# New orders of work for the filling, the steady rounds and the emptying of a three-stage, four-lane decoder kernel

## The chip, the cores and the metric

The kernel runs on one core of one Trainium2 chip. The metric is the device time of the launch in microseconds (us); the kernel before has a median of 3741.29 us over 3 runs (3738.55 to 3749.99). The core has a tensor engine (PE; PEld is its weight load), a vector engine (DVE), a scalar engine (ACT), a GpSimd engine (POOL) and a sync engine (SP) that here only waits, clears semaphores and issues DMAs. Each engine runs its own instructions strictly in order; an instruction that waits on a semaphore holds back all behind it on that engine.

## The reference

32 sequences of 112 tokens with 256 features pass through two pre-norm decoder layers, in fp32. Cut to what matters:

```python
x = x + attn0(layernorm(x))          # 16 heads of 16, 4 key heads, rope, rms norm, tanh-capped causal softmax
x = x + xattn0(layernorm(x), ctx)    # 16 heads of 64 over ctx, causal mask: only ctx rows 0..111 count
x = x + ffn0(layernorm(x))           # 256 -> 1024 gelu -> 256, plus a low-rank term from tokens 1..16
x = x + attn1(layernorm(x))          # 8 heads of 128, latent keys and values of 32
x = x + xattn1(layernorm(x), ctx)    # 16 heads of 16 over 375 ctx rows, with a mask
x = x + moe(layernorm(x))            # 4 experts, top 2 of a gate on the mean over tokens; each expert is a
                                     # whole encoder layer (attention, layernorm, 256->1024->256, layernorm)
```

## The kernel before, in words

**Three stages.** Stage 1 does attn0 and xattn0, stage 2 does ffn0, attn1, xattn1 and the gate, stage 3 first routes (which expert takes which sequence) and then does the 64 expert items. Between stages all engines meet: stage 2 cannot start before the last sequence of stage 1 is done, since weights and buffers are laid over each other.

**Four lanes.** In each stage four lanes work at the same time, called A, B, C and D here (`s` = 0, 1, 2, 3), each with its own buffers, its own two PSUM banks and its own semaphores. A lane does one sequence (a batch) after the other: 8 each in stages 1 and 2, 16 items each in stage 3. Inside a batch nearly every step depends on the one before, and the steps go from engine to engine (a product on PE, a copy or exp on ACT, a mask or a norm on DVE, an inverse root on POOL, and so on). One lane alone therefore leaves each engine idle most of the time; four lanes fill one another's gaps.

**Pieces.** For every engine and stage there is a generator `batch(s, at)`, and each `yield` in it ends a piece: stage 1 has 25 pieces on PE, 19 on ACT, 19 on DVE, 3 on POOL and 4 on SP; stage 2 has 41, 27, 23, 5 and 5; stage 3 has 14, 11, 10, 3 and 4. "A16" on PE is piece 16 of lane A there. Of the pieces that the prediction names: in stage 2 PE 8 and 9 are key products (L892), PE 10 a value product (L827, 8 records), PE 16 the output product of attn1, PE 17 the transposes (L814) that wait for DVE 10 (layernorm's normalise, L1156), PE 19 to 26 the eight pairs of score products of xattn1 (L952), each followed by a masked maximum on DVE (L1232), PE 28 to 35 the second scores (L968, L971), exp on ACT (L1085) and the product with the values, PE 40 the gate. DVE 9 is the residual and layernorm after attn1 and DVE 0 starts the next batch: it waits for `go`, which SP gives after the batch's last DMA has landed. In stage 3 PE 1 is the qkv product (L1465), which waits for the expert's weights (`c_in`); PE 10 and 11 are the first layer of the expert's hidden part, PE 12 and 13 the second (L1536); DVE 0 needs PE 1 and SP's `go_last`, DVE 8 is the layernorm after PE 13, DVE 9 the item's output. SP 2 clears the lane's semaphores after DVE 8, gives `go` and, where the next item has another expert, loads its weights; if not, it only raises `c_in`. SP 3 does the same for `go_last` and the row parameters after POOL 2, the output DMA.

**The order.** `run_slots` (L133) interleaves the pieces of the lanes for one engine. A round has 1000 turns. `TURNS` (L59) gives each piece a turn within its batch, and `lead` says how far ahead each lane is: in stage 1 (0, 250, 500, 750), in stage 2 (0, 341, 505, 677), in stage 3 (0, 262, 500, 762). Turns are only an order: no time is waited for. A hardware loop (`Fori`, count - 1 times: 7, 7 and 15) holds one round of four lanes, starting at the turn 0 of lane A. Before it stands the filling: the same table from turn -750 (stage 1) to 0, so lane D begins alone, C joins at -500, B at -250. Behind it stands the emptying: the same table once more with nothing new begun for the leading lanes, so D ends at turn 250, C at 500, B at 750, and A runs on alone to 1000. Filling and emptying are straight code. Together a stage is filling (1.5 batches of work in stage 1), rounds of 4 batches, and emptying (2.5 batches).

Of the kernel before, what the change touches and what calls it, by code (L numbers as in the profile page):

```python
# [40 lines left out]
def offsets(parts):  # L41
    at, out = 0, {}
    for name, w in parts:
# [17 lines left out]
    "sp1": ((51, 993, 998, 999,),) * 4,  # L61
    "pe1": ((3, 47, 53, 128, 128, 183, 212, 230, 307, 329, 393, 393, 432, 451, 463, 526, 549, 576, 591, 697, 725, 756, 847, 891, 915,),) * 4,
    "act1": ((68, 121, 170, 231, 289, 320, 401, 410, 410, 410, 437, 483, 574, 687, 751, 770, 840, 915, 915,),) * 4,
    "dve1": ((39, 96, 96, 212, 212, 264, 361, 405, 429, 495, 541, 550, 630, 631, 699, 725, 817, 875, 964,),) * 4,
    "pool1": ((79, 276, 739,),) * 4,
# [42 lines left out]
}  # L108


class Tally:


# [12 lines left out]
class Place:  # L126


    def __init__(self, n, last=False):
        self.n, self.last = n, last  # L130


def run_slots(eng, lanes, count, batch, turns, lead):  # L133

# [1699 lines left out]
```

## Time and profile before

| | us |
|---|---|
| median of 3 runs | 3741.29 (3738.55 to 3749.99) |
| the profiled execution | 3746.19 |
| its span, first to last instruction | 3744.5 |
| around the span | 1.7 |
| mean granted TensorE clock | 0.953 of full |
| PE busy | 3393.0 (91%) |
| DVE, ACT, POOL busy | 2125.9 (57%), 1948.2 (52%), 377.1 (10%) |

The profile is one execution. Busy time of PE counts a matmul at the half clock twice as long as at the full one, so it is no measure of work done. Stage 1 lies at 27 to 967 us of the span, stage 2 at 1004 to 2531, the routing at 2531 to 2578, stage 3 at 2578 to the end.

### The profile page before, as it was taken

How to read it: one execution, taken by the hardware profiler on the slowest of the kernel's cores; microseconds unless marked ns; L12 is line 12 of the kernel's file. 1: busy time of each engine (PE TensorE's matmuls, PEld its weight loads, DVE VectorE, ACT ScalarE, POOL GpSimd, SP SyncE). 2: the span in 40 equal slices, each digit the busy share in tenths (PEclk: the TensorE clock that was granted, in tenths of full speed). 3: DMA queues.
4: the chain of work that ended last, by engine and by line, in shares of the span. 5: the costliest groups of instructions: out<-in, count | busy, mean ns of one | idle time of the engine just before them, and what ended most of it. 6: DMA issues, size and time to landing. Idle time of an engine off the chain costs nothing. (4 is left out here: it accounts for less than half of the span.)

```text
span 3744.5 us, 81272 instructions
## 1 busy us (share of the span) xinstructions
PE 3393.0 (91%) x30471; PEld 2533.5 (68%) x30471; DVE 2125.9 (57%) x6898; ACT 1948.2 (52%) x6531; POOL 377.1 (10%) x455
## 2 busy tenths in 40 slices
PE   6999999998699899999999999973999989999997
PEld 4777777776466565656565656633887877877886
DVE  3666666666255454545455554522666666766765
ACT  2555555555144444444444444422666666666664
POOL 1111111111000000000000000000111111111111
PEclk8999999999699999999999999965999999999998
DMA  2000000000200000000000000004000011010000
GB/s 78 13 12 16 12 12 16 12 16 6 90 17 17 21 17 21 17 21 17 23 14 23 14 24 14 7 6 174 15 11 12 16 52 53 16 52 12 16 11 10
DMA packets 63549, 94.38 MB, mean 25 GB/s; under 512 B 7762, under 2 KB 59602, under 8 KB 62146
## 3 DMA queue, kind: packets, MB, share of 16 engines
q1 hardware_dynamic: 55074, 83.41, 7.0%
q0 software_dynamic: 8224, 7.36, 1.7%
q8 instruction: 190, 3.11, 0.3%
q14 instruction: 61, 0.50, 0.0%
HBM read 72.07 MB, written 18.37 MB: 24 GB/s over the span
## 5 line engine op out<-in xcount | busy, mean ns | idle before, releaser
L1232 DVE CUSTOM_DVE_ANT_0 PON<-pps,PMR 112x375 f32<-112x375 f32 x512 | 259.9, 545 | 305.8 <-PE pps L952 304.9
L1465 PE MATMUL bps<-BXT,Bwexp 128*128 128x112 f32 x3072 | 382.2, 283 | 26.7 <-SPq L1386 12.7
L1465 PEld LDWEIGHTS bps<-BXT,Bwexp 128*128 128x128 f32 x3072 | 369.2, 198 | 46.1 <-ACT BXT L1554 16.8
L1571 ACT ACTIVATE BPT<-bps,Blow 112x112 f32<-112x112 f32 x1024 | 346.8, 381 | 38.4 <-DVE Blow L1686 38.4
L1085 ACT ACTIVATE PPT<-pps,mcol 125x896 f32<-125x896 f32 x192 | 193.0, 1005 | 198.9 <-PE pps L971 198.6
L1571 ACT ACTIVATION_READ_ACCUMULATOR BPT<-bps,Blow 112x1 f32 x1024 | 241.1, 235 | 0.0
L952 PE MATMUL pps<-PKT,PQM 64*112 64x375 f32 x1024 | 227.1, 521 | 10.0 <-DVE Pmx L1232 7.9
L1536 PE MATMUL bps<-Bwexp,BPT 128*112 128x256 f32 x1024 | 235.2, 381 | 0.1
L655 POOL TENSOR_TENSOR rstd<-var,nhalf 112x1 f32<-112x1 f32 (+1 forms) x96 | 148.3, 1545 | 771.3 <-DVE var L573 535.2
L1265 POOL TENSOR_TENSOR Prstd<-Pvar,nhalf 112x1 f32<-112x1 f32 x128 | 71.6, 560 | 1450.8 <-DVE Pvar L1152 1450.8
L498 ACT ACTIVATE PT<-PT,low 112x112 f32<-112x112 f32 x512 | 191.2, 387 | 43.5 <-DVE low L630 43.3
L1536 PEld LDWEIGHTS bps<-Bwexp,BPT 128*112 128x112 f32 x1024 | 176.3, 176 | 43.1 <-ACT BPT L1594 3.4
L971 PE MATMUL pps<-PQM,PKT 64*125 64x448 f32 x768 | 195.0, 587 | 0.0
L1160 DVE TENSOR_TENSOR PX<-PX,pps 112x256 f32<-112x256 f32 x96 | 40.3, 420 | 269.4 <-PE pps L827 124.9
L1594 ACT ACTIVATE BPT<-bps,Bwexp 128x112 f32<-128x112 f32 x512 | 140.1, 390 | 70.5 <-PE bps L1465 70.5
L1727 POOL TENSOR_TENSOR Brstd<-Bvar,nhalf 112x1 f32<-112x1 f32 x128 | 78.5, 613 | 895.9 <-DVE Bvar L1658 895.9
L1493 PE MATMUL bps<-BKT,BQM 64*112 64x112 f32 x2048 | 137.7, 275 | 20.9 <-ACT BPT L1571 20.1
L1685 DVE TENSOR_REDUCE Bmx<-bps 112x8 f32<-112x896 f32 x128 | 138.9, 1086 | 13.5 <-PE bps L1493 13.3
L1493 PEld LDWEIGHTS bps<-BKT,BQM 64*112 64x112 f32 x2048 | 114.5, 179 | 47.0 <-ACT BPT L1571 23.3
L1690 DVE TENSOR_TENSOR BPT<-BPT,Brec 112x896 f32<-112x896 f32 x128 | 139.8, 1092 | 4.4
L329 PEld LDWEIGHTS ps<-CT,wa_sb 128*128 128x128 f32 x1024 | 132.3, 206 | 11.1 <-ACT CT L455 1.4
L952 PEld LDWEIGHTS pps<-PKT,PQM 64*112 64x112 f32 x1024 | 76.6, 175 | 91.6 <-issue 64.1
(287 smaller groups left out, 7442.3 us busy)
## 6 DMA issues: line engine op xcount, KB each, us to landing
Bwexp<-in_we SPq DMA_DIRECT2D x7, 2304.0 KB, 13.8
PCX<-in_ctx SPq DMA_DIRECT2D x32, 375.0 KB
BXIN<-xmid SPq DMA_DIRECT2D x64, 112.0 KB
out<-BY POOLq DMA_DIRECT2D x64, 112.0 KB, 2.9
Bwexp<-in_we SPq DMA_DIRECT2D x7, 777.0 KB, 4.5
wa_sb<-in_wa SPq DMA_DIRECT2D x1, 4736.0 KB, 14.4
Brexp<-in_re SPq DMA_DIRECT2D x7, 672.0 KB
XIN<-in_x SPq DMA_DIRECT2D x32, 112.0 KB
```

The lines of the kernel that those rows point to most:

```text
L498: m = A(PT[s][:, h, :], PT[s][:, h, :], ACT.Exp, bias=low[s][:, h:h + 1], accum_out=sums[s][:, h:h + 1])
L655: g.tensor_tensor(rstd[s][:, 0:n], var[s][:, 0:n], nhalf[0:T, 0:n], ALU.pow).then_inc(rstd_ready[s], 1)
L952: m = mm(bank[s][i][0:T, 0:LC], QM[s][side[i], r // 4, r % 4, :], KT[s][side[i], r // 4, :], start=True, stop=True)
L971: m = mm(bank[s][i][0:KP, 0:QW], KT[s][side[i], c, k * KP:(k + 1) * KP], QM[s][side[i], c, :, :], start=False, stop=True, skip_group_check ...
L1085: A(PT[s][0:KP, k, :, :].rearrange("p (i v) q -> p i (v q)", i=2), PS[s][0:KP, :, 0:QW], ACT.Exp, bias=mcol[:, k, bass.ds(at.n[s] + s * qu ...
L1232: m = v.tensor_tensor_reduce(out=ON[s][0:T, i * LC:(i + 1) * LC], in0=bank[s][i][0:T, 0:LC], in1=MR[s][:, :], scale=1.0, scalar=-3.0e38, o ...
L1465: m = mm(o[:, j * T:(j + 1) * T], wt[:, c, n0 + j * 128:n0 + (j + 1) * 128], rhs[:, c, :], start=(c == 0), stop=(c == 1))
L1493: m = mm(bank[s][i][0:T, v * T:(v + 1) * T], QM[s][side[i], c, v, :], KT[s][side[i], c, :], start=True, stop=True)
L1536: m = mm(b0[0:T, 0:D], HT[s][:, mt, :], W(s, "l2", FT)[:, mt, :], start=(mt == 0), stop=(mt == FT - 1))
L1571: m = A(PT[s][0:T, h, :], bank[s][i][0:T, v * T:(v + 1) * T], ACT.Exp, scale=0.25, bias=low[s][:, h:h + 1], accum_out=sums[s][:, h:h + 1])
L1594: m = A(HT[s][:, mt, :], bank[s][g][:, j * T:(j + 1) * T], ACT.Relu, bias=wc(s, "b1")[:, mt:mt + 1])
L1690: v.tensor_tensor(PT[s][0:T, eight, :], PT[s][0:T, eight, :], rec[s][:, eight].unsqueeze(2).to_broadcast((T, 8, T)), ALU.mult).then_inc(so ...
```

## The change

The filling and the emptying get tables of their own, `FIRST` and `LAST`, with places from 0 to 999 over the whole stretch, and all lanes that have work in it take part from its start to its end. `run_slots` walks them in place of the shifted steady table:

```diff
-def run_slots(eng, lanes, count, batch, turns, lead):
+def run_slots(eng, lanes, count, batch, turns, lead, first, last):
...
+    before = [sum(1 for x in turns[s] if x < lead[s]) for s in lanes]
...
-    for turn in range(-SPAN, 0):
-        for s in lanes:
-            local = turn + lead[s]
-            if local >= 0:
-                if local == 0:
-                    runs[s] = [batch(s, at), 0]
-                work(s, local)
+    for s in lanes:
+        if lead[s]:
+            begin(s)
+    for turn in range(SPAN):
+        for s in lanes:
+            if lead[s]:
+                work(s, first[s], turn, before[s])
     with eng.Fori(0, count - 1) as i:
...
-        for s in lanes:
-            local = turn + lead[s]
-            if local == 0:
-                runs[s] = [batch(s, at), 0]
-            if local < SPAN:
-                work(s, local)
+        for s in lanes:
+            work(s, last[s], turn, len(turns[s]))
```

The steady tables are laid out anew, with the same leads. In stage 1 this changes nothing but three neighbouring swaps on ACT: PE, DVE, POOL and SP keep their order of the round. In stages 2 and 3 all engines change: on PE 385 of the 13366 pairs of pieces in a round stand the other way round in stage 2, and 200 of 1540 in stage 3. No instruction is added or removed; a few pieces cross from the loop's edge into the filling (C16 and B8 on PE in stage 2; D1, C0 and D2 on POOL in stage 3).

The orders that the tables give on PE, worked out from them. Emptying of stage 2, the head and the end:

```
before: C16 D24 B8 B9 C17 A0 B10 D25 C18 B11 D26 B12 C19 D27 B13 D28 C20 A1 D29 C21 A2 ... B40 A20 A21 A22 A23 A24 A25 ... A40
after:  D24 B9 A0 A1 A2 A3 B10 A4 A5 A6 A7 B11 A8 B12 A9 B13 A10 A11 C17 D25 A12 C18 ... A38 B37 D39 C39 B38 C40 D40 A39 A40 B39 B40
```

The edge of the loop in stage 2 (the end of a round, then its start):

```
before, PE:  ... A39 D22 A40 B6 D23 B7 | C16 D24 B8 B9 C17 A0 B10 D25      DVE: B4 C9 B5 A0 C10 A1
after,  PE:  ... A39 B6 D23 A40 B7 C16 B8 | B9 D24 B10 C17 A0 B11 D25      DVE: B4 C9 A0 A1 B5 C10
```

The middle of a round in stage 3:

```
before, PE:  C10 C11 B8 C12 C13 A5 D3 C0 B9 C1 B10 B11 A6 B12 B13 D4 C2 A7 B0 C3 A8 B1    DVE: C9 D1 B7 A4 D2 C0
after,  PE:  C10 B8 D2 C11 C12 C13 A5 D3 C0 B9 A6 B10 B11 C1 D4 B12 B13 A7 C2 B0 A8 B1    DVE: C9 C0 D2 D3 B8 B9
```

## Rows read from the trace of the kernel before

**Rows 1.** The page's 40 slices of the span: busy tenths, granted clock.

```profile
PE   6999999998699899999999999973999989999997
...
PEclk8999999999699999999999999965999999999998
```

**Rows 2.** Busy time by stretch: fillings, emptyings, lane A alone; columns stand first.

```profile
core 0: us, PE busy (x) PEld busy (x) DVE busy (x) ACT busy (x) POOL busy (x), PEclk, DMA share, GB/s
27.00:86.20 59.20, 45.90 (x256) 31.82 (x260) 22.45 (x54) 17.00 (x33) 9.28 (x6) 0.83 0.03 10
857.60:966.60 109.00, 86.47 (x710) 65.88 (x709) 51.20 (x212) 50.84 (x176) 9.27 (x6) 0.87 0.02 6
1003.80:1083.80 80.00, 68.94 (x465) 49.81 (x466) 31.46 (x127) 32.12 (x91) 5.85 (x9) 0.91 0.06 18
2366.50:2531.40 164.90, 133.19 (x1156) 77.22 (x1156) 62.91 (x241) 54.73 (x121) 6.44 (x11) 0.79 0.02 7
2577.90:2611.20 33.30, 24.91 (x146) 20.19 (x146) 13.20 (x22) 12.94 (x61) 0.00 (x0) 0.60 0.66 277
3661.00:3743.50 82.50, 61.47 (x510) 52.56 (x510) 40.01 (x97) 37.07 (x149) 9.45 (x14) 0.87 0.07 8
2471.90:2531.40 59.50, 36.29 (x227) 16.79 (x227) 12.39 (x47) 8.29 (x15) 1.10 (x2) 0.53 0.03 8
```

**Rows 3.** Busy time by stretch: one steady round of stages 1, 2, 3, 3.

```profile
780.43:886.96 106.53, 106.29 (x930) 81.71 (x929) 72.91 (x268) 63.39 (x206) 18.53 (x13) 1.00 0.05 13
...
1510.21:1695.12 184.91, 174.75 (x1623) 114.70 (x1621) 94.38 (x369) 85.94 (x212) 12.40 (x20) 0.98 0.07 19
...
2713.12:2782.01 68.89, 64.54 (x626) 55.58 (x625) 47.92 (x109) 46.61 (x200) 8.03 (x12) 1.00 0.08 13
...
3057.64:3132.47 74.83, 66.12 (x626) 57.17 (x625) 47.94 (x110) 46.61 (x200) 8.05 (x12) 0.95 0.22 64
```

**Rows 4.** Timeline of stage 1: POOL's piece 1 of lane B, of A; lane A's end.

```profile
89.03 3.54 POOL L655 TENSOR_TENSOR rstd<-var,nhalf 112x20 f32<-112x20 f32 x1 [15.43 <-DVE var L573]
...
886.96 3.54 POOL L655 TENSOR_TENSOR rstd<-var,nhalf 112x20 f32<-112x20 f32 x1 [16.05 <-DVE var L573]
...
946.53 1.74 PE L417 MATMUL ps<-KX,QT 64*112 64x112 f32 x16 [0.64 <-ACT OT L506]
...
965.50 0.42 DVE L638 TENSOR_TENSOR X<-X,ps 112x256 f32<-112x256 f32 x1 [10.86 <-PE ps L436]
```

**Rows 5.** Timeline of stage 2, POOL: piece 1 of lane A, first and last batch.

```profile
1091.69 0.86 POOL L1272 TENSOR_TENSOR Pcrstd<-Pcvar,nhalf 125x3 f32<-125x3 f32 x1 [2.42 <-DVE Pcvar L1174]
...
2374.43 0.86 POOL L1272 TENSOR_TENSOR Pcrstd<-Pcvar,nhalf 125x3 f32<-125x3 f32 x1 [2.42 <-DVE Pcvar L1174]
```

**Rows 6.** Chain that ended last, stage 3: C10 and C11, first and last loop round.

```profile
2644.23 3.79 PE bps L1465 x32
...
3625.18 3.79 PE bps L1465 x32
```

**Rows 7.** Timeline of stage 2, PE: a steady L952, then lane A alone.

```profile
1625.50 0.89 PE L952 MATMUL pps<-PKT,PQM 64*112 64x375 f32 x4
...
2477.63 1.60 PE L952 MATMUL pps<-PKT,PQM 64*112 64x375 f32 x4 [1.06 <-DVE Pmx L1232]
...
2499.54 1.82 PE L971 MATMUL pps<-PQM,PKT 64*125 64x448 f32 x4
```

**Rows 8.** Timeline at the edge of the loop in stage 2, DVE and PE.

```profile
1633.76 0.42 DVE L1160 TENSOR_TENSOR PX<-PX,pps 112x256 f32<-112x256 f32 x1 [6.19 <-issue]
...
1638.66 0.63 PE L814 MATMUL pps<-const,PXN 112*128 112x112 f32 x2 [5.23 <-DVE PXN L1156]
...
1639.88 3.45 PE L827 MATMUL pps<-Pwa_sb,PCT 128*125 128x256 f32 x8
```

**Rows 9.** Timeline of stage 3, PE: qkv of lane C, then with an expert change.

```profile
2724.45 5.58 PE L1465 MATMUL bps<-BXT,Bwexp 128*128 128x112 f32 x48 [0.92 <-SPq L1386]
...
3073.32 7.14 PE L1465 MATMUL bps<-BXT,Bwexp 128*128 128x112 f32 x48 [5.28 <-DMA Bwexp<-in_we]
```

More of the change, by code:

```diff
@@ L60 @@
     "lead1": (0, 250, 500, 750),
[L61 to L65, printed above, removed]
[42 rows of a table removed]
[62 rows of a table added]
+}
+FIRST = {
[41 rows of a table added]
+            (),
+            (),
+            (820,)),
+    "pe3": ((),
+            (686, 763, 882, 982,),
+            (526, 607, 687, 870, 944,),
+            (236, 298, 399, 602, 745, 933, 973, 973,)),
+    "act3": ((),
+             (734, 885, 923,),
+             (519, 587, 655, 887, 937,),
+             (351, 427, 427, 598, 842, 930, 936, 964,)),
+    "dve3": ((),
+             (743, 886, 968,),
+             (514, 666, 760, 816, 932,),
+             (285, 497, 613, 613, 751, 914, 953,)),
+    "pool3": ((),
+              (),
+              (960,),
+              (878, 935, 961,)),
+}
+LAST = {
[60 rows of a table added]
 }
@@ L130, in __init__, with begin, work, middle @@
         self.n, self.last = n, last
-def run_slots(eng, lanes, count, batch, turns, lead):
+def run_slots(eng, lanes, count, batch, turns, lead, first, last):
     at, runs = Place([0] * len(lanes)), [None] * len(lanes)
-    def work(s, turn):
-        while runs[s][1] < len(turns[s]) and turns[s][runs[s][1]] <= turn:
+    before = [sum(1 for x in turns[s] if x < lead[s]) for s in lanes]
+    def begin(s):
+        runs[s] = [batch(s, at), 0]
+    def work(s, places, turn, end):
+        while runs[s][1] < end and places[runs[s][1]] <= turn:
             next(runs[s][0], None)
             runs[s][1] += 1
-    for turn in range(-SPAN, 0):
-        for s in lanes:
-            local = turn + lead[s]
-            if local >= 0:
-                if local == 0:
-                    runs[s] = [batch(s, at), 0]
-                work(s, local)
-    with eng.Fori(0, count - 1) as i:
+    def middle(i):
         at.n = [i] * len(lanes)
@@ L159, in run_slots @@
                     at.n = [i + 1 if k == s and lead[s] else at.n[k] for k in lanes]
-                    runs[s] = [batch(s, at), 0]
-                work(s, local)
-    at.n, at.last = [count - 1] * len(lanes), True
+                    begin(s)
+                work(s, turns[s], local, len(turns[s]))
+    for s in lanes:
+        if lead[s]:
+            begin(s)
     for turn in range(SPAN):
         for s in lanes:
-            local = turn + lead[s]
-            if local == 0:
-                runs[s] = [batch(s, at), 0]
-            if local < SPAN:
-                work(s, local)
+            if lead[s]:
+                work(s, first[s], turn, before[s])
+    with eng.Fori(0, count - 1) as i:
+        middle(i)
+    at.n, at.last = [count - 1] * len(lanes), True
+    for s in lanes:
+        if not lead[s]:
+            begin(s)
+    for turn in range(SPAN):
+        for s in lanes:
+            work(s, last[s], turn, len(turns[s]))
 def span_of(sems):
@@ L299, in batch @@
                     sp.sem_clear(lane_range[s]).then_inc(go[s], 1)
-                run_slots(sp, LANES, quarter, batch, TURNS["sp1"], TURNS["lead1"])
+                run_slots(sp, LANES, quarter, batch, TURNS["sp1"], TURNS["lead1"], FIRST["sp1"], LAST["sp1"])
                 for s in LANES:
@@ L437, in batch @@
                     m.then_inc(y_psum[s], 1)
-                run_slots(pe, LANES, quarter, batch, TURNS["pe1"], TURNS["lead1"])
+                run_slots(pe, LANES, quarter, batch, TURNS["pe1"], TURNS["lead1"], FIRST["pe1"], LAST["pe1"])
                 for s in LANES:
@@ L663, in batch @@
                     inverse_root(1)
-                run_slots(pool, LANES, quarter, batch, TURNS["pool1"], TURNS["lead1"])
+                run_slots(pool, LANES, quarter, batch, TURNS["pool1"], TURNS["lead1"], FIRST["pool1"], LAST["pool1"])
                 for s in LANES:
@@ L780, in batch @@
                     sp.sem_clear(slot_range[s]).then_inc(go[s], 1)
-                run_slots(sp, LANES, quarter, batch, TURNS["sp2"], TURNS["lead2"])
+                run_slots(sp, LANES, quarter, batch, TURNS["sp2"], TURNS["lead2"], FIRST["sp2"], LAST["sp2"])
                 for s in LANES:
@@ L1002, in batch @@
                     m.then_inc(gate_psum[s], 1)
-                run_slots(pe, LANES, quarter, batch, TURNS["pe2"], TURNS["lead2"])
+                run_slots(pe, LANES, quarter, batch, TURNS["pe2"], TURNS["lead2"], FIRST["pe2"], LAST["pe2"])
                 for s in LANES:
@@ L1099, in batch @@
                     A(lrow[s][:, :], b1[0:1, 0:E], ACT.Copy).then_inc(gate_ready[s], 1)
[L1100 removed]
+                run_slots(act, LANES, quarter, batch, TURNS["act2"], TURNS["lead2"], FIRST["act2"], LAST["act2"])
                 for s in LANES:
@@ L1250, in batch @@
                     normalise(X)
-                run_slots(dve, LANES, quarter, batch, TURNS["dve2"], TURNS["lead2"])
+                run_slots(dve, LANES, quarter, batch, TURNS["dve2"], TURNS["lead2"], FIRST["dve2"], LAST["dve2"])
                 for s in LANES:
@@ L1278, in batch @@
                     inverse_root()
-                run_slots(pool, LANES, quarter, batch, TURNS["pool2"], TURNS["lead2"])
+                run_slots(pool, LANES, quarter, batch, TURNS["pool2"], TURNS["lead2"], FIRST["pool2"], LAST["pool2"])
                 for s in LANES:
@@ L1435, in batch @@
                         load_rows(s, at.n[s] + 1)
-                run_slots(sp, LANES, share, batch, TURNS["sp3"], TURNS["lead3"])
+                run_slots(sp, LANES, share, batch, TURNS["sp3"], TURNS["lead3"], FIRST["sp3"], LAST["sp3"])
                 sp.wait_ge(added, 16 + 64 * share)
@@ L1537, in batch @@
                     m.then_inc(y_psum[s], 1)
-                run_slots(pe, LANES, share, batch, TURNS["pe3"], TURNS["lead3"])
+                run_slots(pe, LANES, share, batch, TURNS["pe3"], TURNS["lead3"], FIRST["pe3"], LAST["pe3"])
             @block.scalar
@@ L1595, in batch @@
                         m.then_inc(h_ready[s], 1)
-                run_slots(act, LANES, share, batch, TURNS["act3"], TURNS["lead3"])
+                run_slots(act, LANES, share, batch, TURNS["act3"], TURNS["lead3"], FIRST["act3"], LAST["act3"])
             @block.vector
@@ L1713, in batch @@
                     v.tensor_scalar(Y[s][:, :], Z[s][:, :], gates[:, bass.ds(at.n[s] + s * share, 1)], None, ALU.mult).then_inc(y_ready[s], 1)
-                run_slots(dve, LANES, share, batch, TURNS["dve3"], TURNS["lead3"])
+                run_slots(dve, LANES, share, batch, TURNS["dve3"], TURNS["lead3"], FIRST["dve3"], LAST["dve3"])
             @block.gpsimd
@@ L1741, in batch @@
                                 accum_op=ALU.add).then_inc(added, 16)
-                run_slots(pool, LANES, share, batch, TURNS["pool3"], TURNS["lead3"])
+                run_slots(pool, LANES, share, batch, TURNS["pool3"], TURNS["lead3"], FIRST["pool3"], LAST["pool3"])
 def _chunks(a):
```

5 lines of the change are left out of this document (2 added, 3 removed), and 201 rows, old and new, of tables (FIRST, LAST, TURNS).

## The prediction, made before the changed kernel was run

> **What bounds the kernel now.** I read the slices first [rows 1]. PE is at nine tenths at full clock except at four places: the start, slices 10 and 11, slices 25 to 27, and the last. Those are the seams of the stages, where lanes join or run out; inside the stages PE is the bound. The windows put numbers on it [rows 3]: a steady round holds PE busy 106.3 of 106.5 us in stage 1, 174.8 of 184.9 in stage 2 and 64.5 of 68.9 in stage 3, so a batch costs PE 26.6, 43.7 and 16.1 us. Nothing done to the order of a round can win more than 0.2, 10.1 and 4.4 us of it.
>
> The seams are found by their turns. In stage 1 POOL's second piece (its place is 276) falls at 89.03 for lane B, which is turn 26, and at 886.96 for lane A's last batch, turn 276 of the emptying [rows 4]; at 106.5 us for 1000 turns, turn 0 is at 86.2 and at 857.6. Stage 2 has the same mark at turn 43 [rows 5]: turn 0 at 1083.8 and 2366.5. In stage 3 C10 comes at turn 479, 33.0 us into a round [rows 6]: the first loop starts at 2611.2 and the emptying at 3625.18 + 68.9 - 33.0 = 3661. So the six stretches last [rows 2]: fillings 59.2, 80.0 and 33.3, emptyings 109.0, 164.9 and 82.5, together 528.9 us, at clocks of 0.60 to 0.91. Their work is 1.5 and 2.5 batches in stage 1, 1.523 and 2.477 in stage 2, 1.524 and 2.476 in stage 3: on a PE that never waits 39.9, 66.6, 24.5 us for the fillings, 66.5, 108.2, 39.9 for the emptyings, 345.6 together. 183 us of the kernel are seams that wait, and the loop's rounds hold the rest.
>
> Why they wait is seen best in stage 2. From 2471.9 on lane A is alone: 59.5 us at a clock of 0.53 [rows 2]. Each of its score pairs takes 1.60 us where a steady one takes 0.89, and PE idles 1.06 for DVE's maximum before it [rows 7]. A chain through four engines sets this stretch, and its idle PE has lost the clock.
>
> **Part 1, emptyings.** No instruction is added or taken away: the gain is that A's chain starts at once ahead of the others' (A0 to A11 before C17) and that B, C and D end beside it. The new length lies between the larger of PE's work and A's chain alone, and today's. I get the chain from lane A alone. In stage 2 its last 375 turns took 59.5 us; at full clock eight pairs save 0.71 each (5.7), six second-score steps half of some 2.5 us of matmuls each, taken from the 1.82 [rows 7] and the small one beside it (7), and half of the other 8.5 of its 36.3 us of PE goes too (4): 43 us, where a steady round spends 375 x 0.185 = 69. That is 0.62. In stage 1 the last 214 turns took 965.9 - 946.5 = 19.4 us [rows 4], some 17 at full clock, against 22.8: 0.75. For a whole batch:
> - Stage 1: 0.75 x 106.5 = 80, above PE's 66.5. With a tenth for collisions 88: **-21** (bounds 80 and 100: -29 to -9).
> - Stage 2: 0.62 x 184.9 = 115, above PE's 108. With a tenth 126: **-39** (bounds 112 and 148, which is four fifths of a round: -53 to -17).
> - Stage 3: no part with A alone is long enough; the nearest is stage 1's 0.75, 52 us, and 8 for the last layernorm, the output and its DMA behind it: 60, **-22** (bounds 50 and 71: -32 to -11).
>
> Sum -82. The other lanes' late ends cost nothing as long as they end before A; in stage 3 the four output DMAs go in the order D, C, B, A, and only A's is last.
>
> **Part 2, fillings.** Here lane D already runs at its own chain's pace with nobody before it; letting B and C in early fills PE but makes D's chain no shorter. What can fall is the time that D waits behind them later, and the clock (0.83, 0.91, 0.60). In stage 1 59.2 us stand against 39.9 of PE's work and 0.75 x 80 = 60 for D's 750 turns by the ratio above: I take 54, **-5**. In stage 2 80.0 against 66.6: 74, **-6**. In stage 3 33.3 against 24.5, with weights still landing (DMA share 0.66): **-2**. Sum -13; bounds 0 and -25, as a chain can eat the whole of it.
>
> **Part 3, the rounds.** Stage 1: same order but for three ACT swaps: 0. Stage 2: at the edge of the loop DVE is idle 6.19 us with no releaser shown, and then PE stands 5.23 us before C17's transposes, which wait for DVE's C10 [rows 8]. The new order puts B10, 3.45 us of PE, ahead of C17, and puts A1 ahead of C10 on DVE, which I price at 2 (a normalise and an add of 0.4 each, three aggregates, and POOL's root that A1 waits for; queued behind it are B5, C10 and with it C17). Net -1.5, seven times: **-10**. Elsewhere neighbours change places under a PE that is busy; I count 0. Bounds for seven rounds: -30 (a good part of the 10 idle us) and +25. Stage 3: PE waits 0.92 a round for SP to raise `c_in` of lane C, and 5.28 where the expert changes, because C1 comes only A5, D3, C0 and B9 (2.8 us) behind C13, whose layernorm lets SP go on [rows 9]. In the new order A6, B10 and B11 also stand between, 4.7 us more. That wipes out the 0.92 fifteen times (14) and most of one reload. Late next are B1, now 3.6 us behind B13 instead of 5.7, and DVE's C0, now right behind C9. I keep half: **-8**, bounds -30 and +30.
>
> SP's and POOL's queues: in stage 3 lane B's XIN load stands behind C's SP 3 instead of before C's SP 2, and POOL's A1 stands after D's output. Both have tens of turns before anyone needs them, so 0.
>
> **Sum.** -82 - 13 - 18 = -113; I keep 106, since the three emptyings share one assumption (the tenth for collisions), and one that errs errs in all. The profiled execution has 3746.2, 1.7 of it around the span, and would become 3640; the median of the runs shown is 4.9 lower, so the forecast is 3741.3 - 106 = **3635**.
>
> **A rule that speaks against.** In the three stretches where several lanes are interleaved thinly the clock is below full: 0.91 with PE busy 86% in stage 2's filling, 0.87 in stage 1's emptying [rows 2]. A new emptying is of that kind for its whole length. If it stayed at the 0.87 and PE's pace set it, stage 2's would take 108.2 / 0.87 = 124 plus the tenth, 137 instead of 126; stage 1's 96, stage 3's 66. That is rival 2. [...]
>
> **Rivals.**
> 1. *Collisions take half.* An order on paper gives each piece its moment; on the chip the engines drift, and a piece of D or C that is not ready holds back A's behind it, in order, on each of four engines. Emptyings then come to their upper bounds nearly, -45 together, and fillings -5. For it: the old emptying of stage 1 ran at steady pace though it had PE to spare. Against: A's pieces stand first. With nothing from the rounds: 3741 - 50 = **3691**. Chance 0.19.
> 2. *The clock stays low*: the gain of the emptyings falls by 11 + 8 + 6 = 25, the others stay: **3660**. Chance 0.12.
> 3. *Slower: stage 3's round gets longer.* In the loop DVE now takes C0 right after C9. C0 waits for `go_last`, which needs POOL's and SP's answer to C9, and for PE's C1, which has moved 4.7 us back; D2, D3, B8 and B9 queue behind it, and D3's maximum feeds the exps that PE's D6 needs. DVE has 21 us idle a round, so mostly this is absorbed. If it is not, it costs those 4.7 plus the 2 to 3 that B8's layernorm is then late: 7 to 8 us in each of 15 rounds. From 7.1 us a round (106 / 15) it decides; at 8, **3755**. Chance 0.08.
> 4. *Nothing to speak of*: lane A's chain under three others is no shorter than now, and the gain is only the half clock of the last 60 us, given back in the rounds: **3735**. Chance 0.05.
>
> **The numbers.** The forecast has 0.56. Faster by over 0.3% (11 us, about what a measurement of this kernel can tell from no change) is the forecast and rivals 1 and 2: 0.87. Same is rival 4: 0.05. Slower is rival 3: 0.08. The range runs from 3580, which is the forecast with the rounds at their lower bounds (-42 more) and 13 of the 32 us that the emptyings' lower bounds still hold, to 3705, past rival 1; outside lie rivals 3 and 4 and a little below.
>
> **What would show it.** Windows from the last `Fori` round to the seam should shrink to about 88, 126 and 60 us, with clocks over 0.9, and lane A's eight score pairs should stand much earlier in the emptying, with B's beside them. The fillings should hardly move. At the edge of the loop in stage 2 PE's idle before L814 should be about 3.7 instead of 5.2; in stage 3 the 0.92 before L1465 x48 should be gone and the round at or under 68.9 us. I am wrong if the rounds of stage 2 or 3 are longer than 184.9 or 68.9, if an emptying still ends with a long stretch of one lane at half clock, or if PE's idle in it is ended by pieces of lanes C and D.

## The result, and the profile after

The changed kernel takes **3577.97 us** (median of 4 runs, 3574.50 to 3584.75) against 3739.92 (4 runs, 3738.49 to 3749.99) of the kernel before on the same chip: a ratio of 0.957, 95% interval 0.955 to 0.959. It is 162 us faster, where 106 were forecast. The profiled execution has a span of 3578.8 us at a mean granted clock of 0.972; 3744.5 and 0.953 before. I account for that difference of spans, 165.7 us.

The slices of the page answer to [rows 1]:

```profile
PE   6999999999799999999999999994999998999998
...
PEclk9999999999799999999999999997999999999999
```

The dips at slices 10 and 11 and at 27 and 28 (the prediction misread their place as 25 to 27) have each shrunk to one slice. Next the busy time by stretch, with the columns of [rows 2]: the filling and the emptying of stage 1, stage 2 from the last A27 in the loop to its end and its last 60 us alone, the filling and the emptying of stage 3, then one steady round of each stage.

```profile
core 0: us, PE busy (x) PEld busy (x) DVE busy (x) ACT busy (x) POOL busy (x), PEclk, DMA share, GB/s
27.00:70.50 43.50, 37.40 (x238) 26.58 (x240) 21.28 (x52) 14.31 (x30) 13.04 (x7) 0.92 0.05 14
845.00:937.70 92.70, 83.78 (x708) 65.23 (x708) 50.88 (x209) 50.39 (x173) 10.06 (x6) 0.93 0.03 7
2290.00:2443.50 153.50, 145.02 (x1516) 94.05 (x1514) 77.16 (x298) 72.62 (x171) 8.16 (x14) 1.00 0.03 8
2490.50:2518.50 28.00, 20.12 (x196) 16.69 (x196) 14.31 (x24) 16.16 (x80) 0.00 (x0) 0.92 0.88 350
3518.00:3577.70 59.70, 47.65 (x434) 40.73 (x430) 36.02 (x89) 30.97 (x122) 9.20 (x14) 0.94 0.09 11
2383.50:2443.50 60.00, 57.58 (x796) 35.13 (x795) 29.30 (x110) 28.80 (x49) 2.30 (x4) 1.00 0.05 14
211.50:323.75 112.25, 109.44 (x930) 84.67 (x929) 72.84 (x268) 64.13 (x206) 18.55 (x12) 0.97 0.05 14
1478.95:1662.31 183.36, 175.71 (x1621) 113.94 (x1620) 94.31 (x369) 85.79 (x212) 12.57 (x20) 0.99 0.07 19
2740.20:2805.55 65.35, 64.35 (x626) 55.72 (x625) 48.00 (x109) 46.50 (x200) 7.79 (x12) 1.00 0.09 14
```

The bounds of the stretches come from marks, as before. Stage 3's loop starts at 2518.5 and ends fifteen rounds later, twelve of 65.36 us and three with an expert change (73.95, 72.65 and 68.43), at 3518.0. In stage 1 the steady order is the old one, and the timeline of POOL has the same marks as [rows 4] (start, length, engine, line, operation, what ended the idle time before it):

```profile
39.66 3.54 POOL L800 TENSOR_TENSOR rstd<-var,nhalf 112x20 f32<-112x20 f32 x1 [8.57 <-DVE var L718]
...
99.99 3.54 POOL L800 TENSOR_TENSOR rstd<-var,nhalf 112x20 f32<-112x20 f32 x1 [16.14 <-DVE var L718]
...
821.02 3.54 POOL L800 TENSOR_TENSOR rstd<-var,nhalf 112x20 f32<-112x20 f32 x1 [16.05 <-DVE var L718]
```

99.99 is lane A's at turn 276, so turn 0 is at 70.5; 821.02 is lane C's at turn 776 of the last loop round, so the emptying begins at 845.0. In stage 2 the order of the round is another, and I compare the same piece, lane A's score step 27, in both kernels. Its mask product (`PMXB`) starts at 1222.00 in the first loop round and at 2327.51 in the last of the kernel before. After:

```profile
1184.81 0.21 PE L1101 MATMUL pps<-constb,PMXB 112*128 112x112 bf16 x1
...
2289.66 0.21 PE L1101 MATMUL pps<-constb,PMXB 112*128 112x112 bf16 x1
```

Here is where the time went (us):

| | before | after | change | forecast |
|---|---|---|---|---|
| stage 1, filling | 59.2 | 43.5 | -15.7 | -5 |
| stage 1, emptying | 109.0 | 92.7 | -16.3 | -21 |
| stage 2, first root to the first loop A27 | 217.6 | 209.7 | -8 | -6 |
| stage 2, last loop A27 to the end | 203.9 | 153.8 | -50 | -39 |
| stage 3, filling | 33.3 | 28.0 | -5 | -2 |
| stage 3, emptying | 82.5 | 59.7 | -23 | -22 |
| six whole rounds of stage 2, A27 to A27 | 1105.5 | 1104.9 | -1 | -10 (seven) |
| a steady round of stage 3, x15 | 68.89 | 65.36 | -50 with the expert changes | -8 |

The seams give -118 where I had -95, and the rounds of stage 3 give -50 where I had -8; that is the larger miss. Stage 1's seven rounds came out 3 longer in this execution, 774.5 us against 771.4, but when the same kernel was run again they did not (run e5: six intervals of lane D take 661.0 us, here 668.0, before 664.6), so that is scatter. Scatter is also 1.8 of the 15.7 us of stage 1's filling: lane D's second root already lies 1.8 us earlier than before, at 39.66 against 41.48, with the same lane alone ahead of it.

Where TensorE waits in one steady round of stage 3 is a short view. Before (what waited, for what, us, times, longest):

```profile
PE bps L1481 <- ACT BKT L1558: 1.0, 1, 1.0
PE bps L1465 <- SPq L1386: 0.9, 1, 0.9
PE bps L1493 <- ACT BPT L1571: 0.9, 1, 0.9
PE bps L1505 <- ACT BPT L1571: 0.8, 1, 0.8
PE bps L1513 <- ACT BPT L1577: 0.7, 1, 0.7
```

These are D2 (the V product), C1 (qkv), C4 (scores), C5 (transposes) and C7 (product with the values), 4.3 us together. After, none of the five is left; one other stands at A5, lane A's transposes:

```profile
PE bps L1650 <- ACT BPT L1716: 0.5, 1, 0.5
```

So 3.8 us of waits went, and the round got 3.5 shorter. I had read one of the five, C1's 0.92. The experiments had three questions: do rounds and seams pay apart from each other; what removed the waits in stage 3; and why did stage 2's round stay at 184.

### The profile page after: what moved, and what is told of

It is laid out like the page before. It is cut to its first block and busy times, and to the rows that moved or that the text cites. A ratio compares the mean times of both kernels' runs of the same rounds, so it can differ in the third digit from the quotient of the medians.

```text
span 3578.8 us, 81208 instructions
## 1 busy us (share of the span) xinstructions
PE 3349.6 (94%) x30471; PEld 2507.5 (70%) x30471; DVE 2125.6 (59%) x6898; ACT 1943.2 (54%) x6528; POOL 375.7 (10%) x455
## 5 line engine op out<-in xcount | busy, mean ns | idle before, releaser
L1610 PE MATMUL bps<-BXT,Bwexp 128*128 128x112 f32 x3072 | 374.4, 279 | 15.1 <-DMA Bwexp<-in_we 7.5
L1610 PEld LDWEIGHTS bps<-BXT,Bwexp 128*128 128x128 f32 x3072 | 360.7, 194 | 36.9 <-ACT BXT L1732 15.9
L1716 ACT ACTIVATION_READ_ACCUMULATOR BPT<-bps,Blow 112x1 f32 x1024 | 250.1, 246 | 0.0
L643 ACT ACTIVATE PT<-PT,low 112x112 f32<-112x112 f32 x512 | 191.0, 384 | 36.3 <-DVE low L775 36.3
L1116 PE MATMUL pps<-PQM,PKT 64*125 64x448 f32 x768 | 187.4, 566 | 0.0
L1722 ACT ACTIVATE BPT<-bps 112x896 f32<-112x896 f32 x128 | 120.5, 941 | 56.6 <-PE bps L1650 56.1
L474 PEld LDWEIGHTS ps<-XT,wa_sb 128*128 128x128 f32 x1024 | 123.8, 198 | 21.4 <-issue 18.8
## 6 DMA issues: line engine op xcount, KB each, us to landing
Bwexp<-in_we SPq DMA_DIRECT2D x7, 2304.0 KB, 15.7
wa_sb<-in_wa SPq DMA_DIRECT2D x1, 4736.0 KB, 14.5
```

Source lines behind the costliest of these rows:

```text
L474: m = mm(bk[:, j * T:(j + 1) * T], wt[:, c, m2 * 128:(m2 + 1) * 128], rhs[:, c, :], start=(c == 0), stop=(c == C2 - 1))
L643: m = A(PT[s][:, h, :], PT[s][:, h, :], ACT.Exp, bias=low[s][:, h:h + 1], accum_out=sums[s][:, h:h + 1])
L1116: m = mm(bank[s][i][0:KP, 0:QW], KT[s][side[i], c, k * KP:(k + 1) * KP], QM[s][side[i], c, :, :], start=False, stop=True, skip_group_check ...
L1610: m = mm(o[:, j * T:(j + 1) * T], wt[:, c, n0 + j * 128:n0 + (j + 1) * 128], rhs[:, c, :], start=(c == 0), stop=(c == 1))
L1716: m = A(PT[s][0:T, h, :], bank[s][i][0:T, v * T:(v + 1) * T], ACT.Exp, scale=0.25, bias=low[s][:, h:h + 1], accum_out=sums[s][:, h:h + 1])
```

## The experiments

### Rounds alone, seams alone (e1, e2)

e1 keeps the new steady tables and cuts filling and emptying from them by the old rule; e2 has the old steady tables with the new seams (but for stage 3's filling, which is cut from the old table). In e1 lane D's row of the emptying in stage 3, for example, is

```diff
     "pe3": (
...
-             (0, 0, 0, 0, 0, 0, 0, 0, 60, 129, 151, 204, 275, 331,)),
+             (0, 0, 0, 0, 0, 0, 0, 0, 17, 27, 42, 49, 134, 134),
```

> This kernel has the new steady rounds in all three stages, and fills and empties each stretch as the kernel before did (the steady order cut short). Theory A (rounds and seams pay apart from each other): only the gain of the rounds stays. By the two traces that is 15 x 3.5 = 53 us of stage 3's rounds, less what its expert changes cost more, nothing of stage 2's, and 3 lost in stage 1's: 3740 - 48 = 3692 us, 3685 to 3700; a round of stage 3 is 65.4 us, the emptyings are 109, 165 and 82 as before. Theory B (the new rounds pay only because the new filling hands them another spacing of the lanes): stage 3's round stays near 68.9 and the time is 3735 to 3745. Theory C (the seams carry everything, the rounds change is offset by expert changes): as B, but with a round of 65.4 and longer waits at the three expert changes.

> The steady rounds of the kernel before in all three stages, with the new fillings and emptyings in stages 1 and 2 and the new emptying alone in stage 3. Theory A (seams pay apart from rounds): stage 1 gives -16 -16, stage 2 -9 -50, stage 3 -25: 3740 - 116 = 3624 us, 3615 to 3640, with stage 3's round at 68.9. Together with the other kernel's -48 that makes the whole -162. Theory B (the emptying is shorter because the new rounds bring the lanes to it nearer together): the emptying of stage 2 stays over 135 us where it is 114 now, and the time is 3650 or more.

Against 3741.40 for the kernel before, **e1 took 3667.89** (3664.93 to 3668.90, 4 runs; ratio 0.980, with a 95% interval of 0.978 to 0.982), that is -74, and **e2 took 3628.91** (3623.77 to 3632.54; 0.970, 0.968 to 0.972), that is -112. Theory A holds for e2 (3624 expected) and is low for e1 (3692). The round of stage 3 is 65.37 us in e1 and 68.90 in e2, with the five old waits back in e2, so the steady tables alone make that difference. Stage 2's emptying in e2 was 49 us shorter than before, with old rounds ahead of it: theory B of e2 falls.

The two sum to -186, 24 more than the change itself. Part of the overlap can be placed. From the output of lane D's second-last item to lane A's last output it is 117.0 us before, 103.0 in e1, 102.7 in e2 and 94.2 in the changed kernel: 14 by either alone, 23 by both, which is 5 of the 24. Another 11 come from stage 2, where e1's rounds took 182.3 us each, 1.8 less than with the new filling ahead of them; the jump of the loop, below, costs less there, but why I did not find out. The other 8 are not placed.

### Which moved piece ended which wait (e3, e4, e7, e8)

The first attempt moved single pieces. e3 puts C1 back in TensorE's new order alone; e4 puts D2 back, and ScalarE's D1 ahead of C8:

```diff
-             (40, 136, 212, 358, 435, 507, 536, 644, 821, 860, 881, 908, 952, 952,),   # pe3, lane C, e3
+             (40, 50, 212, 358, 435, 507, 536, 644, 821, 860, 881, 908, 952, 952),
...
-             (0, 109, 161, 250, 414, 678, 722, 760, 779, 789, 804, 811, 896, 896,)),   # pe3, lane D, e4
+             (0, 109, 118, 250, 414, 678, 722, 760, 779, 789, 804, 811, 896, 896),
...
-             (103, 179, 187, 276, 524, 638, 674, 708, 864, 983, 987,)),                # act3, lane D, e4
+             (103, 170, 187, 276, 524, 638, 674, 708, 864, 983, 987),
```

> The new kernel, but in stage 3's steady rounds TensorE takes lane C's router product (C1) right behind lane B's last piece, as the kernel before did, 86 thousandths of a round before where the change put it. Theory A (stage 3's rounds are shorter because each of five waits of TensorE, 0.92 + 0.90 + 0.79 + 0.71 + 1.02 us, was dissolved by one piece moved): the wait of about 0.9 before C1 is back in every round, the round is 66.2 to 66.4, and the time 3578 + 14 = 3592 us (3585 to 3597). Theory B (the pieces share one slack: what matters is that lane C's chain as a whole got looser): the round stays within 0.2 of 65.36, the time within 4 us of 3578.

> The new kernel, but in stage 3's steady rounds TensorE takes lane D's V product (D2) right behind lane D's scores (D1), and ScalarE takes D1 before C8, as the kernel before did. Theory A (one piece, one wait): TensorE waits about 1.0 us before D2 again, the round is 66.3 to 66.5, the time 3578 + 15 = 3593 us (3586 to 3600). Theory B (shared slack): round within 0.2 of 65.36, time within 4 us of 3578.

e4 took 3582.55 us (3579.78 to 3588.70) and its round 66.12, +0.76: theory A by its round, a little smaller. Its time does not tell the theories apart: it is 5 us above the changed kernel, where fifteen rounds would give 11 and theory A had 15. **e3 took 3663.00** (3658.23 to 3664.49): its round is 71.67, +6.3 where 0.9 was expected. The waits and the window of one round say why:

```profile
PE bps L1475 <- ACT BXT L1564: 4.0, 1, 4.0
PE bps L1515 <- ACT BPT L1581: 0.5, 1, 0.5
```

```profile
2679.31:2750.98 71.67, 66.82 (x626) 58.20 (x625) 48.23 (x109) 46.50 (x200) 7.77 (x12) 0.95 0.08 13
```

C1 does not wait for SP, but 4.0 us for ScalarE's copy C0, which in the new order stands behind lane D's exps (D3). And the granted clock of the round fell from 1.00 to 0.95 (0.50 in the 4.0 us behind this wait, 2692.55 to 2696.50, and 1.00 from 2700.00 on), which made PE's busy time 2.5 us longer. The experiment had put back one engine's half of a neighbourhood.

e7 and e8 went the other way: the kernel before, with pieces spread as the new order has them.

```diff
-             (30, 89, 255, 270, 436, 496, 555, 578, 800, 969, 979, 979, 996, 996,),    # pe3, lane C
+             (30, 89, 255, 270, 436, 550, 605, 640, 800, 969, 979, 979, 996, 996),     # e7
+             (30, 190, 255, 270, 436, 550, 605, 640, 800, 969, 979, 979, 996, 996),    # e8
...
-             (1, 40, 225, 348, 391, 497, 568, 586, 817, 919, 955,),                    # act3, lane C
+             (1, 40, 225, 348, 391, 552, 610, 641, 817, 919, 955),                     # e7 and e8
```

e8 also moves lane D's piece 2, on TensorE from 171 to 242 and on ScalarE from 103 to 192.

> The order of the kernel before everywhere, but for three pieces of lane C in stage 3's round, on TensorE and ScalarE: C5 behind A0, C6 behind D9, C7 behind D13, as the new order has them. Theory A (each wait belongs to one pair of pieces): the waits of 0.79 before C5's scores and 0.71 before C7 go, those of 0.92 (C1), 0.90 (C4) and 1.02 (D2) stay: the round is 68.9 - 1.5 = 67.4 us (67.2 to 67.7), the time 3740 - 22 = 3718. Theory B (slack is shared, TensorE only waits elsewhere): round 68.7 to 69.1, 3740.

> As the one before, and also C1 behind A6 and D2 behind C11 (on ScalarE D2 behind C9): every place where TensorE waited in the old round of stage 3 gets the neighbours that the new order gives it, and nothing else moves; fillings and emptyings are cut from this table. Theory A: the five waits go but for 0.5 to 0.9 before C4, the round is 65.2 to 65.8, near the new one's 65.36, and the time 3740 - 15 x 3.3 = 3690 us (3684 to 3700). Theory B (VectorE's and ScalarE's new orders are needed as well): the round stays above 67.5, the time above 3718.

One run each: e7 3738.56 us with a round of 68.73, **e8 3839.81** with one of 75.7 to 77. Neither is what theory A said. In e7 the waits of C5 and C7 are gone, but two new ones stand at lane D's pieces (waits of one round, the two lines that differ):

```profile
PE bps L1469 <- DVE BPT L1672: 0.7, 1, 0.7
PE bps L1523 <- ACT BPT L1587: 0.5, 1, 0.5
```

They are D9's transposes (L1469) and D7, the product with the values (L1523). In the old order C7 stood ahead of D9 and C5 ahead of B3 and D7; with C5 and C7 moved away, lane D's pieces follow their own predecessors too soon. In e8 TensorE and ScalarE wait, in one round:

```profile
PE bps L1546 <- ACT BPT L1604: 4.3, 1, 4.3
```

```profile
ACT BKT L1568 <- PE bps L1475: 8.1, 2, 7.5
```

C1 had moved on TensorE, and ScalarE's C1 (L1568) stayed where it was: it waited up to 7.5 us for the product, lane B's activations (L1604) stood behind it, and TensorE's second layer behind those. It is e3's lesson from the other side.

### The same put-backs with both engines (e9, e10, e11)

So I undid three groups in the new kernel with the neighbour engine's part included.

```diff
-             (40, 136, 212, 358, 435, 507, 536, 644, 821, 860, 881, 908, 952, 952,),   # pe3, lane C
+             (40, 136, 212, 358, 435, 500, 525, 535, 821, 860, 881, 908, 952, 952),    # e9
+             (40, 50, 212, 358, 435, 507, 536, 644, 821, 860, 881, 908, 952, 952),     # e10
...
-             (31, 140, 190, 360, 415, 534, 636, 839, 914, 942, 942,),                  # act3, lane C
+             (31, 140, 190, 360, 415, 500, 560, 722, 914, 942, 942),                   # e9
+             (31, 33, 190, 360, 415, 534, 636, 839, 914, 942, 942),                    # e10
...
-             (103, 179, 187, 276, 524, 638, 674, 708, 864, 983, 987,)),                # act3, lane D
+             (103, 179, 187, 299, 524, 638, 674, 708, 864, 983, 987),                  # e10
```

e11 has the edits of e9, e10 and e4 together.

> The new kernel, but in stage 3's round lane C's C5, C6 and C7 stand close behind each other again, on TensorE and on ScalarE together (TensorE: C5 A0 D8 A1 C6 B4 D9 C7, where the new order has C6 and C7 after D9 and after D13). Theory A (in the new order TensorE finds other lanes' work while ScalarE does the piece between; put back, the old waits of 0.79 and 0.71 return): round 65.36 + 1.0 to 1.5 = 66.4 to 66.9 us, time 3578 + 19 = 3597. Theory B (what shortened the round is C1's and D2's place alone): round within 0.2 of 65.36, 3578.

> The new kernel, but in stage 3's round C1 stands right behind B9 on TensorE, as in the run e3, and this time ScalarE takes C0 and C1 before D3, as the kernel before did. Theory A (e3's 6.3 us a round were not C1's place but ScalarE's copy C0, which stood behind lane D's exps while TensorE waited for it): the round comes down from 71.7 to 66.0 to 66.5, with the old 0.92 before C1 back, and the time is 3578 + 14 = 3592 us. Theory B (C1's place itself is what counts): round over 69.

> The two put-backs of e9 and e10 together with that of e4 (D2 right behind D1). Theory A (the old round's five waits belong to five pairs of pieces of one lane, each put back alone): the sum of the three, 65.36 + 1.25 + 0.9 + 0.76 = 68.3 us (67.8 to 68.9), close to the old 68.89; time 3578 + 44 = 3622 us. Theory B (the waits share slack): clearly less than the sum of the three, round under 67.5.

| | round of stage 3 | above 65.36 | time |
|---|---|---|---|
| e4, D2 back | 66.12 | 0.76 | 3582.55 |
| e9, C5 to C7 back | 66.41 | 1.05 | 3589.92 |
| e10, C1 back, both engines | 66.36 | 1.00 | 3594.23 |
| e11, all three | 68.17 | 2.81 | 3614.70 |

(e9 to e11 are one run each; a round is the distance of one lane's outputs without an expert change between, the same to 0.04 us within a run.) The three alone sum to 2.81, and together they cost 2.81. Theory A holds in its sum: the costs of the three groups add, and they share nothing. The times rose by 12, 16 and 37 us for e9 to e11 against 3577.97, where fifteen rounds give 16, 15 and 42. e10 against e3 shows that ScalarE's order had cost 5.3 of e3's 6.3 us: same place for C1, 66.36 against 71.67. The waits of a round in e11:

```profile
PE bps L1475 <- ACT BXT L1564: 1.1, 1, 1.1
PE bps L1491 <- ACT BKT L1568: 0.6, 1, 0.6
PE bps L1503 <- ACT BPT L1581: 0.5, 1, 0.5
PE bps L1515 <- ACT BPT L1581: 0.5, 1, 0.5
PE bps L1515 <- DVE BPT L1700: 0.5, 1, 0.5
```

By their places in the order they are C1, D2, B4 (scores), A5 (transposes, the one that the changed kernel has too) and B6 (transposes), 3.2 us together. They are those of e4, e9 and e10 put together, but of the old five only D2's is back with its old releaser, at 0.6 us where it had 1.0. C1 waits for ScalarE's copy C0 here, where the old C1 waited for SP; and with C5 to C7 back the waits stand at B4 and B6, not at C5 and C7. So the put-backs show what these places are worth in the new order, 2.8 of the 3.5 us; which piece ended which old wait is shown for D2 alone. The 0.7 us that still lie between 68.17 and the old 68.89 I did not place. Nor did I try one engine's whole old order against the new orders of the others; I took it that the engines would wait for each other in a circle.

### The jump of the loop (e5, e6, e12)

```diff
-    with eng.Fori(0, count - 1) as i:
-        middle(i)
+    if count == 8:
+        for i in range(count - 1):
+            middle(i)
+    else:
+        with eng.Fori(0, count - 1) as i:
+            middle(i)
```

Stages 1 and 2 have a count of 8, stage 3 of 16. e5 is the changed kernel itself once more, e6 the same with this edit, e12 the kernel before with it.

> The changed kernel itself once more, on the chip of the three kernels sent with it. Its first profile has stage 1 end 7 us later than two other kernels with the same stage 1 had it. Theory A (that is chance: clock dips fall differently from run to run): median 3570 to 3585 us, with stage 2's first root at 968 to 976 us. Theory B (it belongs to this program): 975 again.

> The changed kernel with the seven rounds of stages 1 and 2 written out as straight code in place of the hardware loop; stage 3 keeps its loop. Theory A (what is lost in a stage-2 round, 184.1 us at a granted clock of 0.98 against 180.2 in the one undisturbed round of the old profile, is the jump back: 3.2 us of TensorE and 3.0 of VectorE idle with no releaser, and the clock that dips behind it): each of six inner turns saves 3 to 4 us in stage 2 and 2 to 4 in stage 1, 3578 - 40 = 3538 us, 3520 to 3555, with no idle marked as issue of over 1 us in the rounds. [...]

> The kernel before with the rounds of stages 1 and 2 written out as straight code, as e6 did for the new one. Theory A (the jump back costs both kernels about the same, and hid nothing): stage 1's round 106.2 as in e6, stage 2's 178 to 180, where e6 has 177.66; the time 3743 - 65 = 3678 us, 3665 to 3695, and the change is worth 3678 - 3509 = 169, as with the loops. Theory B (the new order of stage 2's round is really shorter and the jump hides it): stage 2's round stays over 181, the time over 3700.

e5 took 3576.58 us (3571.13 to 3581.54) and has stage 2's first root at 967.07: scatter, theory A. **e6 took 3509.10** (3506.48 to 3511.30; ratio to the kernel before 0.937, 0.936 to 0.939), 67 less than e5, more than theory A had. e12 took 3660.32 (3658.85 to 3667.54; 0.978, 0.976 to 0.980), 85 less than the 3745.49 of the loop. Neither theory of e12 had that: its round of stage 2 is 175.15 us, under the 178 to 180 of theory A. With the loops written out the change is worth 151 us (e12 against e6), not 169. The rounds, in the windows of e6, two of stage 2 and two of stage 1:

```profile
1257.92:1435.58 177.66, 173.78 (x1622) 113.23 (x1621) 94.28 (x369) 85.65 (x212) 12.73 (x20) 1.00 0.07 20
1435.58:1613.24 177.66, 173.78 (x1622) 113.23 (x1621) 94.26 (x369) 85.64 (x212) 12.54 (x21) 1.00 0.08 20
343.36:449.51 106.15, 106.15 (x930) 81.78 (x929) 72.77 (x268) 63.62 (x206) 18.54 (x12) 1.00 0.05 15
555.66:661.81 106.15, 106.15 (x930) 81.78 (x929) 72.86 (x268) 63.62 (x206) 18.54 (x12) 1.00 0.05 14
```

and of e12, stage 2:

```profile
1470.88:1646.04 175.16, 172.47 (x1623) 113.43 (x1621) 94.31 (x369) 86.00 (x212) 12.39 (x20) 1.00 0.08 20
1646.04:1821.19 175.15, 172.47 (x1623) 113.42 (x1621) 94.37 (x369) 86.04 (x212) 12.39 (x20) 1.00 0.08 20
```

These rounds no longer scatter, they are at full clock (1.00), and in stage 1 TensorE never waits at all (busy 106.15 of 106.15 us). Seven rounds have six jumps back. With the loop, e5's six intervals of lane D's root in stage 1 took 661.0 us, without it e6's took 636.9: **4.0 us a jump**. In stage 2 it is 1104.5 against 1066.0: **6.4 us a jump** in the new order, and in the old one (1105.5 before, 175.15 each in e12) **9.1**. A part of it is marked idle; the timeline of TensorE behind a jump in e5 shows the rest:

```profile
1590.12 2.84 PE L1037 MATMUL pps<-PCT,Pwa_sb 128*128 128x375 f32 x4 [3.14 <-issue]
1592.89 1.60 PE L1097 MATMUL pps<-PKT,PQM 64*112 64x375 f32 x4
1594.42 2.35 PE L972 MATMUL pps<-Pwa_sb,PCT 128*125 128x256 f32 x8
1596.60 0.74 PE L959 MATMUL pps<-const,PXN 112*128 112x112 f32 x6
1597.27 0.89 PE L1097 MATMUL pps<-PKT,PQM 64*112 64x375 f32 x4
```

After 3.1 us in which the profile shows nothing to wait for, the four products of L1037 take 2.84 us, where such four take 1.53 later in the same round, and the four score products behind them take 1.60 us instead of 0.89. The granted clock is 0.50 from 1590.12 to 1594.40, 0.87 from 1594.42 to 1597.27 and 1.00 in the 7.7 us after that, where four score products take 0.89 again. Behind the other five jumps of stage 2 in e5 it is 0.50 to 0.60 in the first 4.2 to 4.3 us, in stage 1 0.50 to 0.67 behind four of the six and 1.00 behind the last two. In e6 and e12 TensorE has no idle left in stages 1 and 2 that no releaser explains, where e5 has 15.6 us in stage 1 and 19.5 in stage 2, in six places each. So the idle goes when the jump goes; what takes the time inside the jump no run shows. It was 4.0 to 9.1 us a jump here.

And so the new round of stage 2 is **2.5 us longer** than the old one, 177.66 against 175.15, and its jump 2.7 cheaper. These two hid each other.

### The old round of stage 2 in the new kernel, and stage 3 unrolled (e13, e14)

e13 is e6 with stage 2's steady tables (five engines) of the kernel before, between the new filling and emptying. e14 has stage 3 as straight code too, that is `middle(i)` for every stage.

> The new kernel with stages 1 and 2 written out as straight code (as e6), and in stage 2 the steady round of the kernel before between the new filling and the new emptying. Theory A (the new order makes stage 2's round itself 2.5 us longer, and the jump back, which costs the old order 9.1 us and the new one 6.5, hid that): stage 2's round is 175.2 us, the time 3509 - 17 = 3492 us (3486 to 3498). Theory B (the 2.5 us come with the new filling, which hands over other spacings of the lanes): round over 177, time 3505 to 3512.

> The same, with stage 3's fifteen rounds written out as well. Theory A (stage 3's round shows only 0.5 us of idle that is a wait for ScalarE, and TensorE runs at full clock across the jump, so the jump is hidden there): the round stays at 65.3 to 65.4 and the time within 4 us of the run before it, or some 10 us worse if straight code takes longer to come than a loop of this length. Theory B (the jump costs a little in every engine's stream, not marked): round at or under 64.9, 8 us or more off the time.

**e13 took 3494.74 us** (3490.58 to 3499.84, 5 runs; ratio 0.934, 0.932 to 0.937), its round of stage 2 is 175.15: the 2.5 us belong to the round. **e14 took 3489.82** (3487.62 to 3496.31, 6 runs; 0.933, 0.931 to 0.936). Its round of stage 3 is 65.18 instead of 65.35, 2.5 us over fifteen. That is between the theories, and the 5 us between the medians lie in the scatter. Both are faster than the changed kernel by over 80 us, and are the best versions that I found.

## Why the prediction was right or wrong

- **That the emptyings carry the gain, by moving lane A's chain ahead of the others: right as far as the seams go.** e2, with new seams and old rounds, has 112 of the 162 us. The last 60 us of stage 2, 36.3 us of work at a clock of 0.53 before [rows 2], now hold 57.6 us of work at 1.00. The lengths came out near, 59.7 against the 60 of stage 3 and 92.7 against the 88 of stage 1, but that is in part luck: the 60 took its ratio from stage 1 and 8 us from no row (from VectorE's last residual to the end of the stage, which the 8 stood for, it is 9.8 us in both traces, 3733.66 to 3743.5 and 3567.88 to 3577.7), and the 88 is a chain of 80 with the tenth for collisions. In these stretches no single wait of TensorE is over 2 us, so that it is A's chain which sets their length is argued, not shown.
- **"With a tenth for collisions 126" in stage 2: too careful.** By its 50 us the emptying is 115, if turn 0 stands as far behind A27 as before (39 us). TensorE is busy 145.0 of the last 153.5 us; there was no tenth. This is +11 us of gain. Rival 1 (collisions take half) falls: the emptyings gave 89 us, not 45. Rival 2 (the clock stays low) falls for stages 2 and 3, where the clock is 1.00 and 0.94 and the stretches are no longer than forecast. In stage 1 it is 0.93, up from 0.87, and 92.7 us lie between the forecast's 88 and the rival's 96, so there it is open. The rival's sum was wrong besides: at a clock of 0.87 and PE's pace with the tenth stage 1 comes to 84 us and stage 3 to 50, not 96 and 66, so that only stage 2's 11 us follow from it. The clock below full in thinly interleaved stretches, which I had weighed against the change, did not come in the last 153.5 us of stage 2, at 1.00.
- **"D's chain no shorter" in the fillings, 0.75 x 80 = 60 us in stage 1: wrong.** The 0.75 is lane A's last quarter, and does not carry over to lane D's first three. The row that would have told stood in the trace of before, ahead of those of [rows 4]: lane D's second root, when it was alone:

```profile
41.48 3.54 POOL L655 TENSOR_TENSOR rstd<-var,nhalf 112x20 f32<-112x20 f32 x1 [12.64 <-DVE var L573]
```

  It has place 276 of lane D's table and came 14.5 us after the start at 27.0, where 276 turns of a steady round take 29. A lane alone ran its first quarter in half the time; its other 474 turns, with lanes C and B joining in the old places, took 44.7 us, near the 50.5 of a steady round. In the new filling they take 30.8. So D could win more than the 5 us: the filling took 43.5 us with TensorE busy 37.4 in it. Miss: 11 us, of which 1.8 are scatter.
- **"Elsewhere neighbours change places under a PE that is busy; I count 0": the step that failed in both rounds.** In stage 3 I read one wait of five and kept 8 us of it, and set the bound at -30, which the lower edge of the range, 3580, rests on; the measured -50 lies outside it. The sum of the round's idle was in [rows 3], 68.9 - 64.5 = 4.4, and the waits view lists its five parts; each stood where one lane's pieces followed each other with a step of ScalarE or SP between. The new order puts other lanes' pieces there. By e1 and e2 it is the steady tables alone that make it: 65.37 against 68.90 us a round. By e4, e9, e10 and e11 the places of D2, C5 to C7 and C1 are worth 0.76, 1.05 and 1.00 a round, 42 us in fifteen rounds, and all of the changed places 3.5, or 53 less the 2 to 3 that the reloads at the expert changes gave back. Miss: 42 us. That SP's 0.92 would go was right; what the new order does about each of the other four is shown only for D2.
- **The edge of stage 2's loop, -10: right in kind, and cancelled.** The jump became 2.7 us cheaper, 16 us in six; the rest of the round 2.5 us longer, 17.6 in seven. I had counted the second as 0 too. What I called the edge's 6.19 and 5.23 us of idle [rows 8] was not a wait of order, but the jump: with the loop written out (e12) VectorE has no idle without a releaser in the round, and the wait before the same transposes, there L820, is down from 5.23 to 0.4 us:

```profile
PE pps L820 <- DVE PXN L1162: 0.4, 1, 0.4
```

- **The 7 us held back** (113 summed, 106 forecast) made the miss larger by as much. With the smaller terms, emptying of stage 1 -5, fillings of stages 2 and 3 +5, emptying of stage 3 +1, edge of stage 2 -9 and stage 1's rounds -3, that accounts for the 60 us between 165.7 and 106.
- **Rival 3 (stage 3's round longer by DVE's C0): did not happen.** The round is 65.36 with TensorE busy in 64.35. Its mechanism exists elsewhere: e3's round is 6.3 us longer than the changed kernel's, and e8's 6.8 to 8.2 longer than the old one, since one engine's piece stood ahead of work that it held back.

## What to carry to other kernels

A steady order is judged by the waits view of one round. Every wait between two pieces of one lane is a place to try other lanes' work. Undone one by one in the new order, three such places added up exactly; put into the old order, one of them (e7) won 0.16 us of the 1.5 expected, since the waits moved to the pieces that had lost their neighbours. So the waits are read again after each move. And a piece is moved on all engines that touch it or not at all: half a move cost 6.3 us in a round of 65, the whole one 1.0. Before an order is tuned around the edge of a hardware loop, write the loop out once: here the jump cost 4.0 to 9.1 us, made the rounds scatter (in stage 2 of the kernel before six of them took 180.2 to 186.0 us, written out in e12 two took 175.15 and 175.16) and hid that a new order was longer.

## What the runs showed of the hardware

- At the jump back of the loops of stages 1 and 2 (930 and 1621 matmul records a round) TensorE is idle with no releaser, 2.3 to 2.8 us in stage 1 and 2.9 to 3.9 in stage 2 of e5, and VectorE 3.0 us in mean in stage 2. Behind it TensorE's granted clock was 0.50 to 0.67 for some 4 us, but for the last two jumps of stage 1, where it was 1.00. Together that cost 4.0 us in stage 1, 6.4 or 9.1 in stage 2, by the order of the round. The loop of stage 3, with 626 matmul records a round, costs some 0.2 (65.35 against 65.18 us). With straight code in all three stages (e14) TensorE has no idle without a releaser, and VectorE none over 0.4 us. The cost is not a fixed one. In stage 2 the old round costs 9.1 behind the old filling and 9.0 behind the new one (e2); the new round costs 4.6 behind the old filling (e1, 182.3 us a round) and 6.4 to 6.5 behind the new one. So the order of the round matters, but e1 and the changed kernel have the same loop body, and their difference is not that of the instructions at the edge. Its cause is open.
- With 4.0 us of TensorE idle at one place of a round (e3) the granted clock was 0.50 in the 4.0 us behind it and 0.95 in the mean of the round. Idle that is spread as 0.5 to 1.1 us in five places (e11, 68.2 us with 64.6 of work) left it at 1.00.
- The first root of 20 columns in stage 1 lies at 39.4 to 45.2 us in the kernels that have the new filling, and at 39.66 and 41.52 in two executions of the changed kernel itself, so single executions can't be compared to better than that without such marks.
